# Batch 0's convolution moved right behind its own top-k tiles, with its feed-forward beside the last four top-k tiles of batch 1

## The chip, the cores and the metric

One Trainium2 chip, one of its cores. The time is the device time of one execution in microseconds (us); lower is better.

## The reference

The model is two attention blocks and two expert blocks on a text of two batches of 1024 rows by 256 channels and a context of two batches of 77 rows by 192. Cut to what matters here (the first attention and the first expert block, called A and B below, are not touched except for B's last step):

```python
x = x + xattn0(x, ctx)                       # A: 16 heads
x = x + experts0(x)                          # B: top 2 of 8, gated, projected by Wo
# C: 4 heads over 77 keys, the 32 largest scores of each row kept
scores = einsum(Q, K) / sqrt(32)
topv, topi = top_k(scores, 32); probs = softmax(topv)
c_t = attn.mean(heads) @ V                   # FiLM: scale and shift in and out
u = layernorm(x);  x_in = u * (1 + scale_in) + shift_in
# D: long convolution over the 1024 rows, by Fourier transform
y = irfft(rfft(x_in) * rfft(K)) + x_in * D_skip
# FiLM out, layernorm, then E: gelu(h @ W1 + b1) @ W2 + b2, layernorm, residual
# F: y = x @ w_expert + b ; gate by the largest of 8 logits, at most 100 rows per expert
```

(The names are shortened; the layer norms and residual sums around each block are as in the reference.)

## The kernel before

The kernel is written engine by engine: one list of instructions for each of PE (tensor), DVE (vector), ACT (scalar), POOL (gpsimd) and SP (DMA issue). Each list runs strictly in its written order, and waits on semaphores where it needs another engine's result. So the order of the calls in a list is the schedule, and an instruction whose wait has not come holds up all that stands behind it.

The 2048 rows are 16 tiles of 128 rows, 8 for each batch (`TB = 8`), and four blocks of 512 rows. All matrix products are in f32. The steps that the change and the prediction speak of, with their lines:

- End of B: for each tile, ACT takes half of a sum of two gathered expert rows (`half_sum`, L1229), DVE the other half (`sum_gated`, L1679), PE turns it (`turn_sum`, L778) and multiplies by `wof` (`out_B`), ACT copies the turned tile in between (`put_sumT`), and DVE adds it to X (`add_B`, L2083). These run `LEAD = 6` tiles ahead of the top-k loop.
- Preparation of C: PE makes four small products for the FiLM rows, then four for the keys (`wqk`); ACT copies the keys and DVE scales the FiLM rows (`film_rows`).
- C for tile n: PE `turn_u`, `scores`; DVE `top_k` as four rounds of `top_eight`, each of four MAX8 (L2137) and four MATCH_REPLACE8 (L2141), the end of the first round being a small L2148; ACT `exp_all` (L1272) and `exp_top_and_rest` (L1279, L1284); POOL `weights` (L1591 to L1604), which begins by inverting the sums of exponentials; PE `turn_attn` (L814) and `film_in`; ACT `put_attn` and `put_film`; POOL `x_in` (L1610, L1612).
- The spectrum of the convolution's kernel: 8 steps of PE `kernel_spectrum`, ACT `put_kernel`, DVE `kernel_pair` (L2154), through one PSUM bank, one step in each of the iterations 1 to 8.
- D for batch b: DVE `fold` (L2172); PE `spectra(b, pair)`, 8 products of 128x512; ACT `put_spectra`; DVE four `product` calls; PE `inverse(b, pair)`; DVE `unfold` (L2225); then PE `film_pair` and DVE `film_add` for each pair of tiles, which alternate; DVE `stats_E`, POOL `rstd_E`, ACT `norm_E`, PE `turn_E`.
- E for block i: PE `hidden(i, f)`, f = 0 to 7, ACT `gelu` (L1355), PE `out_E` for four tiles, DVE `add_E` and `norm_E`. Before E, PE makes `b1_folded` (16 products of one column) for the bias, once.
- F for block i: DVE `stats_F`, `norm_F`; PE `expert_F` (`turn_F`, `out_F`); ACT `put_zTF`; DVE `back_F`. Then the gate and the stores.

In the kernel before, batch 0's convolution is spread over the iterations 9 to 15 of the top-k loop. Block 0 of E follows the loop, then batch 1's convolution between the blocks 0 and 1, then the blocks 2 and 3 with the experts F of the blocks 0 and 1 beside them. In `weights(n)` POOL inverts four sums of exponentials as a power of -1:

```python
own.done(p.tensor_tensor(q_[:, 1, :], q_[:, 0, :], negone[:], ALU.pow))
```

## Time and profile before

| what | value |
|---|---|
| median of 3 runs | 857.21 us (855.03 to 858.87) |
| the profiled execution's own time | 865.67 us |
| span of the profiled execution | 863.6 us |
| mean granted TensorE clock | 0.886 of full speed |
| busy: PE, DVE, ACT, POOL | 690.4, 539.8, 343.3, 390.9 us |

The span is what the engines' instructions cover; the profiled execution took 2.1 us more than its span. A stretch of the profile gives for each engine its busy time and count, then the granted clock of TensorE as a share of full speed. PE's busy time is the time in which a product was under way, so a slower clock makes it larger. In the timeline each row has a start, a duration, the engine, the line, and in brackets how long the engine had stood idle before and whose result it had waited for. f32 products stand as two or more records each.

### The profile page before, as it was taken

Reading aid. Unit: us, or ns where it says so; the run is one execution under the profiler, and the core shown is the slowest. Engines: PE = TensorE matmul, PEld = TensorE weight load, DVE = VectorE, ACT = ScalarE, POOL = GpSimd, SP = SyncE. Lnnn points to the kernel's source line nnn. Section 1 sums busy time; section 2 is a strip of 40 time slices with the busy share of each in tenths; the row PEclk is TensorE's granted clock in tenths of the full one; section 3 lists DMA queues with packets and bytes.
Section 4 is the critical chain, followed back from the end, with each engine's and each line's share of the span. In section 5 each row is a group of like instructions: output and inputs, shape, how many; then the busy total and the mean of one; then the engine's idle time right before and its main releaser. Section 6 shows DMA issues by size and latency. Waiting matters only on the chain.

```text
span 863.6 us, 10795 instructions
## 1 busy us (share of the span) xinstructions
PE 690.4 (80%) x3380; PEld 387.4 (45%) x3380; DVE 539.8 (63%) x1641; ACT 343.3 (40%) x776; POOL 390.9 (45%) x448
## 2 busy tenths in 40 slices
PE   4798888369998989895688997827858997999972
PEld 2344455334454544442454544313513742657661
DVE  4889884749948393601568878598263476654165
ACT  2565553216373828210356765433334121042210
POOL 4666341238887877610126667655332410123020
PEclk9989998569999999986789999877757998999987
DMA  8920010211222222205930004000000000000002
GB/s 217 392 59 2 0 65 25 73 43 62 86 80 73 89 67 86 86 26 167 362 129 1 1 1 147 1 0 1 0 1 0 1 0 0 2 0 1 1 0 97
DMA packets 33215, 52.78 MB, mean 61 GB/s; under 512 B 8846, under 2 KB 21710, under 8 KB 32904
## 3 DMA queue, kind: packets, MB, share of 16 engines
q1 hardware_dynamic: 28168, 36.76, 12.9%
q0 software_dynamic: 4992, 15.34, 5.3%
q8 instruction: 28, 0.46, 0.2%
q14 instruction: 27, 0.22, 0.1%
HBM read 36.62 MB, written 15.47 MB: 60 GB/s over the span
## 4 chain that ended last, share of the span: by engine, by line
PE 47%; DVE 31%; ACT 10%; issue 6%; POOL 2%; DMA 1%; POOLq 1%; SPq 0%; DVEq 0%; ACTq 0%
PE ps L479 44%; DVE arena L1673 6%; DVE kp L1673 4%; DVE arena L1790 3%; DVE arena L1786 3%; DVE arena L1776 2%; ACT arena L1037 2%; ACT arena L1121 2%; DVE arena L2141 2%; ACT L1194 1%; DVE arena L2137 1%; DVE arena L2025 1%; DVE arena L340 1%; ACT L1208 1%; DVE arena L1676 1%
## 5 line engine op out<-in xcount | busy, mean ns | idle before, releaser
L479 PE MATMUL ps<-arena 64*32 64x32 f32 (+6 forms) x2280 | 480.9, 400 | 42.6 <-ACT arena L1037 11.7
L479 PEld LDWEIGHTS ps<-arena 128*128 128x128 f32 (+4 forms) x2280 | 221.9, 153 | 235.0 <-issue 172.9
L1037 ACT ACTIVATE arena<-ps 128x512 f32<-128x512 f32 (+4 forms) x228 | 108.1, 496 | 199.1 <-PE ps L479 114.3
L2025 DVE TENSOR_TENSOR arena<-ps,arena 128x512 f32<-128x512 f32 x39 | 26.9, 689 | 85.6 <-ACT arena L1194 77.4
L335 POOL TENSOR_SCALAR rstd<-mv 128x1 f32<-128x1 f32 (+1 forms) x24 | 10.8, 450 | 132.5 <-DVE mv L329 104.7
L1535 POOL DMA_INDIRECT scr_g<-arena,destU x39 | 48.8, 1252 | 44.1 <-DVE arena L2025 35.0
L1493 POOL TENSOR_TENSOR arena<-arena 128x616 f32<-128x616 f32 x32 | 39.0, 1217 | 50.5 <-DVE arena L1778 50.4
L1526 POOL DMA_INDIRECT arena<-scr_z,idsU x39 | 49.5, 1270 | 22.9 <-PE ps L708 11.6
L1673 DVE TENSOR_TENSOR arena<-arena 128x1024 f32<-128x1024 f32 (+10 forms) x47 | 40.3, 858 | 29.8 <-issue 18.5
L1194 ACT ACTIVATE arena<-ps 128x512 f32<-128x512 f32 x39 | 23.3, 598 | 83.7 <-PE ps L479 83.6
L2141 DVE MATCH_REPLACE8 arena<-arena 128x77 f32<-128x77 f32 x256 | 54.1, 222 | 0.0
L2137 DVE MAX8 arena<-arena 128x8 f32<-128x77 f32 x256 | 41.7, 224 | 16.7 <-POOL arena L1604 12.3
L1355 ACT ACTIVATE arena<-ps,b1p 128x512 f32<-128x512 f32 x32 | 22.0, 688 | 60.5 <-PE ps L479 60.5
L1591 POOL TENSOR_TENSOR arena<-arena,negone 128x4 f32<-128x4 f32 x16 | 21.7, 1354 | 53.9 <-ACT arena L1279 53.9
L479 PE MATMUL ps<-arena,wq 128*128 128x308 f32 (+1 forms) x104 | 40.0, 510 | 4.7 <-ACT arena L1037 4.1
L1121 ACT ACTIVATE arena<-arena 128x616 f32<-128x616 f32 x32 | 22.9, 717 | 45.5 <-DVE arena L1790 45.4
L479 PE MATMUL ps<-b1r,picked 72*128 72x512 bf16 x78 | 30.6, 393 | 8.7 <-DVE arena L2025 4.6
L479 PE MATMUL ps<-wof,arena 128*128 128x256 f32 x128 | 35.3, 425 | 0.6 <-DVE X L2083 0.5
L1673 DVE TENSOR_TENSOR arena<-arena,kp 128x1024 f32<-128x1024 f32 (+1 forms) x32 | 34.6, 1102 | 0.3
L1610 POOL TENSOR_TENSOR arena<-arena 128x256 f32<-128x256 f32 x16 | 12.8, 800 | 47.3 <-ACT arena L1037 47.3
L1776 DVE TENSOR_REDUCE arena<-arena 128x8 f32<-128x616 f32 x32 | 25.3, 791 | 13.4 <-ACT arena L1121 12.5
L814 PE MATMUL ps<-ident,arena 128*77 128x128 f32 x16 | 5.4, 335 | 33.7 <-POOL arena L1604 33.6
(215 smaller groups left out, 1096.8 us busy)
## 6 DMA issues: line engine op xcount, KB each, us to landing
arena<-in_w1t SPq DMA_DIRECT2D x8, 1024.0 KB, 14.7
arena<-scr_g SPq DMA_DIRECT2D x14, 512.0 KB, 5.9
X<-in_x SPq DMA_DIRECT2D x2, 1024.0 KB, 6.2
scr_z<-arena SPq DMA_DIRECT2D x4, 512.0 KB, 2.8
arena<-in_c_dftf SPq DMA_DIRECT2D x1, 2048.0 KB, 14.1
arena<-in_L_xattn_W SPq DMA_DIRECT2D x2, 1024.0 KB, 6.3
out<-X SPq DMA_DIRECT2D x16, 128.0 KB, 1.8
scr_k<-arena SPq DMA_DIRECT2D x4, 256.0 KB, 5.8
```

What stands on the lines that cost most here:

```text
L479: return pe.matmul(o, l, r, start=first, stop=final)
L1037: return a.activation(o, i, ACT.Copy)
L1121: a.activation(Pb[:, S % PBUF, :], Pb[:, S % PBUF, :], ACT.Exp, scale=1.0 / math.sqrt(DH0))\
L1194: a.activation(sig[:, u % 2, :], bank(2 * (u % 2) + 1), ACT.Sigmoid).then_inc(s["sig_ready"], 1)
L1493: p.tensor_tensor(pv, pv, smA[:, u % PBUF, :].unsqueeze(2).broadcast_to([P, HG, S2]), ALU.mult)\
L1526: p.indirect_dma_start(xg[:, st % 2, :], None, scr_z, bass.IndirectOffsetOnAxis(ap=idsU[:, st:st + 1], axis=0))\
L1535: p.indirect_dma_start(scr_g, bass.IndirectOffsetOnAxis(ap=destU[:, u:u + 1], axis=0), gt[:, u % 2, :], None).then_inc(s[f"gs{u % 2}"], 16)
L1673: own.done(v.tensor_tensor(o, x, y, op))
L1776: own.done(v.tensor_reduce(smA[:, u % PBUF, :], Pb[:, u % PBUF, :].rearrange("p (h k) -> p h k", h=HG), AX, ALU.add))
L2025: v.tensor_tensor(gt[:, u % 2, :], bank(2 * (u % 2)), sig[:, u % 2, :], ALU.mult).then_inc(s["g_ready"], 1)
L2137: own.done(v.max(top[:, par, h, 8 * r:8 * r + 8], hv(cur)[:, h, :]))
L2141: ins = v.match_replace(hv(Rr)[:, h, :], top[:, par, h, 8 * r:8 * r + 8], hv(cur)[:, h, :], TAKEN)
```

## The change

It changes the order of the calls on PE, ACT, POOL and DVE from the end of B on, and moves buffers and PSUM banks so that the new order has no clash:

- PE's loop goes over the tiles 0 to 9 and the rest is written out. `kernel_spectrum(n)` stands in iteration n (0 to 7), behind `turn_attn(n-1)`. Tiles 12 to 15 of B's end (`EARLY = 12`) come after tile 8's top-k.
- After tile 10's top-k come all four products of batch 0 in a row, then tile 11, unfold and FiLM of batch 0; block 0 of E runs beside the top-k of the tiles 12 to 14, block 1 beside tile 15 and ahead of batch 1's convolution.
- F of the blocks 0 and 1 stands between batch 1's spectra. ACT, not DVE, takes F's results from PSUM (`put_yF`), and POOL adds the bias (`bias_F`).
- The inverse of the sums of exponentials moves from POOL (`negone`, pow) to DVE (`invert`, a reciprocal of 128x4), which signals `ex_inv`.
- On ACT the first two `half_sum` stand ahead of the copies of `wqk`.
- `hidden` goes round three PSUM banks instead of two, and `xT` has two buffers.

```diff
@@ tensor @@
                 for n in range(NT):
                     if n + 1 < NT:
                         scores(n + 1)
-                    if n + LEAD + 1 < NT:
+                    if n + LEAD < EARLY:
                         turn_sum(n + LEAD + 1)
-                    if n + LEAD < NT:
                         out_B(n + LEAD)
-                    if 1 <= n <= 8:
-                        kernel_spectrum(n - 1)
                     if n:
                         turn_attn(n - 1)
+                    if n < 8:
+                        kernel_spectrum(n)
...
+                    if n == 8:
+                        out_B(EARLY)
+                        turn_sum(EARLY + 1)
+                        out_B(EARLY + 1)
                     if n == 9:
                         spectra(0, 0)
...
+                        break
+                turn_sum(EARLY + 2)
+                out_B(EARLY + 2)
+                turn_attn(9)
+                scores(11)
+                film_in(9)
+                turn_sum(EARLY + 3)
+                out_B(EARLY + 3)
+                spectra(0, 1)
+                turn_attn(10)
+                film_in(10)
+                inverse(0, 0)
+                turn_u(12)
+                scores(12)
+                b1_folded()
+                inverse(0, 1)
...
@@ scalar @@
+                half_sum(0)
+                half_sum(1)
                 for b in range(NB):
                     for g in range(2):
                         a.wait_ge(s["prepC_ps"], 8 + 2 * b + g)
                         copy(wqk[:, g, b, :], bank((4, 5, 1, 7)[2 * b + g], SW)).then_inc(s["prepC_sb"], 1)
-                half_sum(0)
-                half_sum(1)
...
+                for n in range(8):
                     exp_all(n)
+                    put_scores(n + 1)
+                    if n + LEAD < EARLY:
                         put_sumT(n + LEAD + 1)
                         half_sum(n + LEAD + 3)
                     if n:
                         put_attn(n - 1)
+                    if n in (2, 6):
+                        norm_u(n // 4 + 1)
+                    exp_top_and_rest(n)
+                    put_kernel(n)
                     if n:
                         put_film(n - 1)
+                    put_uT(n + 2)
...
+                exp_all(12)
+                gelu(0, 0)
+                gelu(0, 1)
+                put_scores(13)
+                put_uT(14)
+                gelu(0, 2)
+                gelu(0, 3)
+                exp_top_and_rest(12)
+                exp_all(13)
+                gelu(0, 4)
...
@@ gpsimd @@
                 def weights(n):
 
                     q_, E = smC[:, n % 2], Ex[:, n % 2, :]
-                    p.wait_ge(s["ex_sum"], n + 1)
-                    own.done(p.tensor_tensor(q_[:, 1, :], q_[:, 0, :], negone[:], ALU.pow))
-                    own.settle()
+                    p.wait_ge(s["ex_inv"], n + 1)
...
@@ vector @@
+                def invert(n):
+
+                    v.wait_ge(s["ex_sum"], n + 1)
+                    v.reciprocal(smC[:, n % 2, 1, :], smC[:, n % 2, 0, :]).then_inc(s["ex_inv"], 1)
+
+                for n in range(8):
+                    top_k(n, (0, 1))
+                    if n + LEAD + 2 < EARLY + 2:
                         sum_gated(n + LEAD + 2)
+                    if n:
+                        invert(n - 1)
+                    top_k(n, (2, 3))
+                    if n + LEAD < EARLY:
                         add_B(n + LEAD)
+                    kernel_pair(n)
+                top_k(8, (0, 1))
+                sum_gated(14)
+                invert(7)
+                add_B(12)
+                top_k(8, (2, 3))
+                sum_gated(15)
+                add_B(13)
+                kernel_ends()
+                invert(8)
+                top_k(9, (0, 1))
+                fold(0)
+                top_k(9, (2, 3))
+                top_k(10, (0, 1))
+                invert(9)
+                top_k(10, (2, 3))
+                add_B(14)
+                invert(10)
+                product(0, 0, 0)
+                add_B(15)
+                product(0, 0, 1)
+                product(0, 1, 0)
+                product(0, 1, 1)
...
```

How the instructions stand. First PE in one iteration of the loop (`L778` or `L780` is turn_sum, `wof` out_B, the row of 128x512 x4 is kernel_spectrum, `L814` or `L816` turn_attn, `L796` or `L798` turn_u, `L479` arena 128x512 alone film_in, `onerow` and `wq` scores). Before:

```order
L479 MATMUL ps<-arena,onerow 128x308
L479 MATMUL ps<-arena,wq 128x308 x2
L778 MATMUL ps<-ident,arena 128x128 x4
L479 MATMUL ps<-wof,arena 128x256 x4
L479 MATMUL ps<-arena 128x512 x4
L814 MATMUL ps<-ident,arena 77x128
L796 MATMUL ps<-ident,arena 128x128 x2
L479 MATMUL ps<-arena 128x512
```

and of the change:

```order
L479 MATMUL ps<-arena,onerow 128x308
L479 MATMUL ps<-arena,wq 128x308 x2
L780 MATMUL ps<-ident,arena 128x128 x4
L479 MATMUL ps<-wof,arena 128x256 x4
L816 MATMUL ps<-ident,arena 77x128
L479 MATMUL ps<-arena 128x512 x5
L798 MATMUL ps<-ident,arena 128x128 x2
```

The four products of the kernel's spectrum now stand behind turn_attn, and film_in follows them directly (five products of 128x512 in a row).

Second, DVE in one tile of the loop in the change (`L2291` and `L2295` are the top-k rounds, `L1833` sum_gated, `L2407` invert, `L2237` and `L2239` add_B, `L2308` kernel_pair):

```order
L2302 TENSOR_SCALAR arena<-arena 128x4
L2291 MAX arena<-arena 128x8 x4
L2295 MATCH_REPLACE arena<-arena 128x77 x4
L1833 SCALAR_TENSOR_TENSOR arena<-arena,cw 128x512
L2407 RECIPROCAL arena<-arena 128x4
L2291 MAX arena<-arena 128x8 x4
L2295 MATCH_REPLACE arena<-arena 128x77 x4
L2291 MAX arena<-arena 128x8 x4
L2295 MATCH_REPLACE arena<-arena 128x77 x4
L2237 TENSOR_TENSOR X<-X,ps 128x256
```

The inverse for tile n-1 stands behind two rounds of tile n, and kernel_pair, which stood between the rounds 3 and 4, is now the last of the tile.

Third, ACT beside block 0 of E in the change (`L1407` is gelu, `L1333` and `L1338` exp_top_and_rest, `L1326` exp_all):

```order
L1326 ACTIVATE arena<-arena 128x77 x4
L1407 ACT_TABLE_LOAD
L1407 ACTIVATE arena<-ps,b1p 128x512 x2
L1317 ACTIVATE arena<-ps 128x308
L1091 ACTIVATE wq<-ps 128x256
L1407 ACTIVATE arena<-ps,b1p 128x512 x2
L1333 ACT_TABLE_LOAD
L1333 ACTIVATE arena<-arena 128x32 x4
L1338 ACTIVATE arena<-arena 128x77 x4
L1326 ACTIVATE arena<-arena 128x77 x4
L1407 ACT_TABLE_LOAD
```

Gelu and exponentials now alternate. From tile 12 on seven loads of a table stand between them, where before there was one.

## Rows read from the trace of the kernel before

**Rows 1.** Page: busy time of each engine; the chain that ended last; gathers to landing
```profile
PE 690.4 (80%) x3380; PEld 387.4 (45%) x3380; DVE 539.8 (63%) x1641; ACT 343.3 (40%) x776; POOL 390.9 (45%) x448
...
PE 47%; DVE 31%; ACT 10%; issue 6%; POOL 2%; DMA 1%; POOLq 1%; SPq 0%; DVEq 0%; ACTq 0%
...
arena<-scr_g SPq DMA_DIRECT2D x14, 512.0 KB, 5.9
```

**Rows 2.** Windows: PE, PEld, DVE, ACT, POOL busy (count), PE clock, DMA share, GB/s
```profile
480.00:500.00 20.00, 19.08 (x67) 10.39 (x65) 17.12 (x126) 13.16 (x51) 12.43 (x22) 1.00 0.00 1
560.00:580.00 20.00, 7.22 (x22) 3.17 (x20) 19.90 (x67) 6.99 (x25) 10.07 (x10) 0.78 0.00 0
...
620.00:640.00 20.00, 12.72 (x32) 7.21 (x32) 10.94 (x56) 4.96 (x16) 5.42 (x9) 0.50 0.01 1
```

**Rows 3.** Timeline of ACT before the loop: copies of wqk, then the first half sums
```profile
412.38 1.98 ACT L1037 ACTIVATE arena<-ps 128x308 f32<-128x308 f32 x4 [10.11 <-PE ps L479]
414.26 1.32 ACT L1229 ACTIVATE arena<-arena,cw 128x512 f32<-128x512 f32 x2
```

**Rows 4.** Timeline of DVE before the loop: sums 0 and 1, sum 2, first round of top-k
```profile
415.00 1.41 DVE L1679 SCALAR_TENSOR_TENSOR arena<-arena,cw 128x512 f32<-128x512 f32 x2 [13.07 <-ACT arena L1229]
...
424.66 0.75 DVE L1679 SCALAR_TENSOR_TENSOR arena<-arena,cw 128x512 f32<-128x512 f32 x1 [0.22 <-DVE arena L1676]
...
445.76 0.66 DVE L2137 MAX8 arena<-arena 128x8 f32<-128x77 f32 x4 [4.31 <-ACT arena L1263]
```

**Rows 5.** Timeline of PE before the loop: the products for the FiLM rows
```profile
402.32 9.50 PE L479 MATMUL ps<-arena 128*77 128x512 f32 x16 [0.39 <-ACT arena L1037]
```

**Rows 6.** Timeline of DVE in the loop: tile 2's rounds, ends of round 1, tile 7's kernel_pair
```profile
460.93 0.63 DVE L2137 MAX8 arena<-arena 128x8 f32<-128x77 f32 x4
...
463.76 0.74 DVE L1679 SCALAR_TENSOR_TENSOR arena<-arena,cw 128x512 f32<-128x512 f32 x1
...
472.32 0.16 DVE L2148 TENSOR_SCALAR arena<-arena 128x4 f32<-128x4 f32 x1
...
481.54 0.16 DVE L2148 TENSOR_SCALAR arena<-arena 128x4 f32<-128x4 f32 x1
...
534.76 0.41 DVE L2154 TENSOR_TENSOR arena<-ps,arena 128x256 f32<-128x256 f32 x1
```

**Rows 7.** Timeline of POOL in the loop: first and last step of weights behind the inverse
```profile
477.21 0.30 POOL L1593 TENSOR_SCALAR arena<-arena 128x4 f32<-128x4 f32 x1
...
479.71 0.32 POOL L1604 TENSOR_TENSOR arena<-arena 128x77 f32<-128x77 f32 x1
```

**Rows 8.** Timeline of PE: kernel_spectrum, turn_attn, b1_folded, a film_pair at low clock
```profile
477.17 3.60 PE L479 MATMUL ps<-arena 128*128 128x512 f32 x8
480.61 0.27 PE L814 MATMUL ps<-ident,arena 128*77 128x128 f32 x1
...
618.00 6.83 PE L479 MATMUL ps<-gb_ffn,arena 128*128 128x1 f32 x32
...
629.95 3.78 PE L479 MATMUL ps<-arena 97*128 97x512 f32 x4 [1.50 <-DVE kp L2235]
```

**Rows 9.** Groups of ACT behind 445 us, forms apart: copies of 128x256, mean ns
```profile
L1037 ACT ACTIVATE arena<-ps 128x256 f32<-128x256 f32 x40 | 15.2, 379 | 44.0 <-PE ps L928 27.1 <-PE ps L479 16.9
```

**Rows 10.** Timeline of DVE: fold(0), first and last step of two products of batch 1
```profile
531.09 2.36 DVE L2172 TENSOR_TENSOR arena<-arena 128x1024 f32<-128x1024 f32 x2 [1.88 <-POOL arena L1612]
...
717.97 1.23 DVE L1673 TENSOR_TENSOR arena<-arena 128x1024 f32<-128x1024 f32 x1 [6.71 <-issue]
...
729.64 0.69 DVE L2215 TENSOR_TENSOR arena<-arena,kp 128x512 f32<-128x512 f32 x1
```

**Rows 11.** Timeline of ACT in block B: a table load between two functions
```profile
250.85 0.38 ACT L1037 ACTIVATE arena<-ps 128x256 f32<-128x256 f32 x1
251.25 1.28 ACT L1208 ACT_TABLE_LOAD   x1
252.54 1.06 ACT L1208 ACTIVATE arena<-arena 128x1024 f32<-128x1024 f32 x1
```

602 lines of the change are left out of this document (343 added, 259 removed).

## The prediction

> **What bounds the kernel now.** I read the page first: PE is busy for 80% of the span but holds only 47% of the chain that ended last, DVE 31% [rows 1]. So there are stretches of two kinds, and the windows tell them apart [rows 2]. In the top-k loop (480 to 500 us) PE is busy 19.1 of 20 us at full clock: PE is the bound. From about 550 to 655 us it is not. At 560 DVE is busy 19.9 of 20 us with batch 0's products while PE has 7.2, and at 620 PE's granted clock is 0.50 (its 1.2 GHz level). The change aims at this second stretch. Whether it pays depends on what the new order does to the first. So I took the timelines and followed, in each engine's new list, which wait ends last, with durations from the rows.
>
> **The change, part by part.** Times are in the profiled execution, whose span is 863.6 us (its own time is 865.67, 1% above the median of 857.21; I carry the difference in us over to the median).
>
> *Ahead of the loop: a gain of 8 us.* ACT copies the keys at 412.4, when PE has made the last of its eight products, and only then takes the first half sums at 414.3 [rows 3]. DVE therefore starts its sums 0 and 1 at 415.0, and its FiLM rows stand behind them: sum 2 comes at 424.7 [rows 4]. With the half sums first, they need only the first gathers, which land 5.9 us after their issue [rows 1], at about 405. DVE then does the FiLM rows while PE still makes them (402.3 to 411.8 [rows 5]), and should be through at 416.3. The first round of top-k moves from 445.8 [rows 4] to about 437.5.
>
> *The loop: a new ring of waits, 11.3 us a tile in place of 9.2.* Before, a tile takes 481.54 - 472.32 = 9.2 us [rows 6], about PE's work. In the change this ring closes:
> - DVE ends kernel_pair(n-1), the last of its tile, and does two rounds of tile n: 463.76 - 460.93 = 2.83; sum_gated 0.7 [rows 6]; then invert(n-1), which I take at 0.25 (no such row; the small L2148 takes 0.16 [rows 6], and twice my value is the upper end).
> - POOL's weights(n-1) without the power: 477.21 to 480.03, 2.82 [rows 7].
> - PE's turn_attn(n-1), 0.2 until the next can start, and behind it kernel_spectrum(n), 3.60 [rows 8].
> - ACT's copy 0.38 [rows 9], DVE's kernel_pair(n) 0.41 [rows 6], and some 0.2 for the handoffs.
>
> The sum is 11.35 us. Before, kernel_spectrum stood ahead of turn_attn and waited for no weights. Seven turns of the ring give 79.4. The first tile has about 10.5 us (two exponential groups stand ahead of its copy), norm_u in two of the tiles adds 1.9, and the tiles 6 and 7, which have no gated sum, give back 1.4. Tile 7's kernel_pair then ends 90.2 us after the first round, at 527.7. Before it ended at 535.2 [rows 6], but with tile 8's top-k and half of tile 9's behind it, and with four steps of B that now still stand ahead. The power that POOL no longer takes is no gain here: its place in the ring is taken by two rounds of top-k.
>
> *From there to block 0 of E: 107 us.* I count from tile 7's kernel_pair.
> - Tile 8: DVE's add_B(12) waits for out_B(12), which stands behind turn_attn(7) and film_in(7): 11.2. Its other two rounds end at 14.9. ACT's put_sumT(13) is behind tile 8's exponentials, so out_B(13) ends at 21. kernel_ends and two rounds of tile 9 take it to 26.7, fold 2.36 [rows 10] to 29.3.
> - PE's spectra(0,0), 6.9 at full clock, come after a nearly idle stretch: 9.5, to 38.8. Then put_sumT(14), out_B(14), turn_attn(9), scores, film_in(9), put_film and tile 10's sum stand in one line over ACT and PE: invert(10) at 48.6.
> - Four products. Two with one op of 0.4 between them span 717.97 to 730.33, so 6.0 each [rows 10]. With add_B(15) and a wait of 0.4 they end at 74.2.
> - PE: inverse(0,0) to 71, scores, b1_folded 6.8 [rows 8] to 79, inverse(0,1) 6.9 to 86, unfold to 89.3. Tile 11's top-k is hidden in it.
> - film_pair and film_add alternate four times. A pair takes 1.8 at full and 3.78 at the 1.2 GHz level [rows 8], an add three ops of 0.69 like the last of a product [rows 10]. With stats_E, norm_E and turn_E ahead of the last pair that is 17.7 at a mean between the levels. `hidden(0)` starts at 107, at 634.7 us.
>
> *The blocks 0 and 1 of E: 66.4 us to out_E(4), then 52.2 us to the last product of batch 1.* PE has 18.2 us of work in block 0's hidden part, but ACT's list has norm_E(1), the exponentials of tiles 12 and 13 and three table loads in it: 26.4. Block 1 stands twice behind put_attn, which is behind a gelu. The six added loads cost 1.28 each, at once behind the op before and with the next at once behind them [rows 11], so 7.7 in all, nearly all of it in ACT's full stretches. The Trainium skill, "ScalarE: Activation LUTs", section "Table sets: the hidden batching unit", gives the rule to batch calls by table set, which speaks against this interleaving. Its section on the cost states 2.66 us for a switch with its drain, by which six would be 16 us; here a load with both neighbours spans 1.31, so the sum goes by 1.28.
> Then out_E(4 to 7) 15, spectra(1,0) 7, and the products, which wait for put_spectra(1,1) behind the third yf_ready: the last ends 225.6 after tile 7's pair, at 753.3. Before it ended at 730.3 [rows 10], but with out_E(4 to 7) and the experts F of the blocks 0 and 1 still to do.
>
> *The end: 121.2 us in place of 133.3.* inverse(1,0) stands behind expert_F(1), so 9.8 to its end, unfold, four film pairs with PE nearly idle: hidden(2) 28 after the last product. Blocks 2 and 3 with expert_F(2) take 62.3. The tail from the last out_E I put at 31, some 5 shorter than before, since F's last block no longer queues behind DVE's back_F of the block before.
>
> *Sum:* 437.5 + 90.2 + 107 + 66.4 + 52.2 + 121.2 = 874.5, or 10.9 over 863.6. On the median: **868 us**.
>
> **Costs at nothing.** POOL's added bias_F, a sum of 128x256 each, runs while ACT and PE do the next tile; only if rstd_E(2) queued behind the first eight would it cost, up to 3 us. Waiting for the table of the Fourier transform with the kernel's (`k_in`) is hidden: it was issued at 412 and POOL asks for it behind 434.
>
> **The rivals.**
> - *The order holds PE busy (faster).* If PE's clock stays at 2.4 GHz from 550 on and the table loads fall into ACT's waits, the sum loses 15 (low clock: spectra 2.6, out_B 2, inverses and b1 3, film pairs 4 + 3) and 8: 851.5, on the median 845. For it: PE has some 59 us of work in the 107 and 91 in the 118 after. Against: in the like stretch before the clock was 0.78 and 0.50 [rows 2], and the film pairs leave PE half idle. The break-even with before is at 11 of these 23 us.
> - *Half of that (no change):* only the clock or only the loads: 853 to 861, hardly any of it above.
> - *The loop throttles as well (slower still).* In the ring PE works 8.8 (19.1 / 20 of 9.2 [rows 2, 6]) of 11.3 us. If the clock fell there, kernel_spectrum at 1.2 GHz would add up to 3.4 to a turn; over half the tiles that is 12: 880. Against: the gaps are short.
> - *The ring doesn't bind,* because weights(n-1) is ready sooner than I read. Then the loop keeps 9.2 a tile, 15 us less: 853. The written order leaves no way for it that I see.
>
> **How the numbers follow.** The sum as it stands, with its walk uncertain by some 9 us: 0.50. PE held busy: 0.18. Half of it: 0.15. The loop throttled too: 0.11. Ring not binding: 0.06. The range reaches from 845, the first rival, to 882, which takes in the third rival and invert at twice its cost; about 2 in 10 lie outside. A measurement of this kernel tells 0.5% (4.3 us) from no change, so slower means over 861.5, faster under 852.9. The sum's case puts 0.40 above, 0.07 between and 0.03 below; with the rivals: slower 0.53, same 0.20, faster 0.27.
>
> **What would show it.** Right: kernel_pair rows 11.3 us apart, each waiting for ACT's copy; the first MAX8 of the loop at about 437; seven table loads between gelu and exponentials; hidden(0) at about 635; the last product of batch 1 at about 753; a clock well under 1.00 between 535 and 640. Wrong: kernel_pair rows 9 us apart, or a clock of 0.95 and more from 550 to 640, or a last product before 740.

## The result, and the profile after

The change takes **898.52 us** (median of 4 runs, 897.92 to 902.57; a fifth execution on record took 907.14) beside 856.12 us for the kernel before: ratio 1.052, 95% interval 1.046 to 1.058. The prediction said 868 us with a range to 882. The direction was right and the size was not: 42 us were lost, not 11.

The profiled execution, page: busy times, granted clock in 40 slices, the chain that ended last.

```profile
PE 699.5 (78%) x3380; PEld 389.0 (43%) x3380; DVE 534.4 (59%) x1625; ACT 360.4 (40%) x814; POOL 383.9 (43%) x448
...
PEclk9999996589999999969899877976789897889986
...
PE 45%; DVE 30%; ACT 14%; issue 5%; POOL 4%; DMA 1%; POOLq 1%; SPq 0%; DVEq 0%; ACTq 0%
```

Against [rows 1] nearly no work was added (PE 9 us, ACT 17), the span grew by 37, and what gained in the chain is ACT, from 10% to 14%. So time was lost in waits, and ACT is in them.

First a correction of the scale. The last step ahead of stage C is a drain of POOL's DMA queue. The chain of waits before, then after:

```profile
390.79 7.66 POOLq L320
```

```profile
381.24 7.65 POOLq L320
```

Stage C began at 398.5 before and at 388.9 in the change, though nothing ahead of it is altered. In 14 of the 19 profiles of this study it begins between 388.6 and 391.9, in the other five (before, ring_open2, warm_all, no_tables, before_warm) between 398.5 and 409.3. In these five the granted clock from 360 to 380 was 0.74 to 0.92, in the others 1.00. The last four ran on one chip, on which the kernel before took 867.43 us and not 856 to 857, so a late stage C isn't the kernel's doing. The profile before was a late one, which is why its own time stood 1% above its median. I therefore count **from the start of stage C** (the end of that drain). From there the span is 465.1 us before and 511.8 in the change: 46.7 more. A second profile of the change (run `again`) gave 512.0, every landmark of it within 2.2 us. How far a single profile can be trusted stands under `again`.

Ahead of the loop, timelines of ACT (half sums, then the copies of wqk) and DVE (sums 0 and 1, first round of top-k), against [rows 3, 4]:

```profile
394.40 1.34 ACT L1283 ACTIVATE arena<-arena,cw 128x512 f32<-128x512 f32 x2 [1.68 <-DMA arena<-scr_g]
402.24 1.98 ACT L1091 ACTIVATE arena<-ps 128x308 f32<-128x308 f32 x4 [6.51 <-PE ps L479]
```

```profile
395.15 1.42 DVE L1833 SCALAR_TENSOR_TENSOR arena<-arena,cw 128x512 f32<-128x512 f32 x2 [2.78 <-ACT arena L1283]
...
426.60 0.66 DVE L2291 MAX8 arena<-arena 128x8 f32<-128x77 f32 x4 [5.21 <-ACT arena L1317]
```

The first round comes 37.7 us behind the start of C (426.6 - 388.9), before 47.3: a gain of 9.6.

In the loop, DVE's kernel_pair of the tiles 4 to 7:

```profile
485.63 0.42 DVE L2308 TENSOR_TENSOR arena<-ps,arena 128x256 f32<-128x256 f32 x1 [3.63 <-ACT arena L1091]
496.96 0.43 DVE L2308 TENSOR_TENSOR arena<-ps,arena 128x256 f32<-128x256 f32 x1 [3.21 <-ACT arena L1091]
510.45 0.42 DVE L2308 TENSOR_TENSOR arena<-ps,arena 128x256 f32<-128x256 f32 x1 [7.24 <-ACT arena L1091]
524.02 0.42 DVE L2308 TENSOR_TENSOR arena<-ps,arena 128x256 f32<-128x256 f32 x1 [7.32 <-ACT arena L1091]
```

They wait for ACT's copy, as forecast, and two of the turns are 11.33 us to the hundredth. But the last two are 13.5, the first three 12.9, 12.3 and 13.0, and the mean over all seven is (524.02 - 436.15) / 7 = 12.55. PE's rows tell why: turn_attn with its wait, and behind it kernel_spectrum and film_in, in a fast turn and in a slow one.

```profile
492.74 0.34 PE L816 MATMUL ps<-ident,arena 128*77 128x128 f32 x1 [1.89 <-POOL arena L1727]
492.91 4.46 PE L479 MATMUL ps<-arena 128*128 128x512 f32 x10
...
503.43 0.49 PE L816 MATMUL ps<-ident,arena 128*77 128x128 f32 x1 [3.41 <-POOL arena L1727]
503.72 7.15 PE L479 MATMUL ps<-arena 128*128 128x512 f32 x10
```

The same ten records take 4.46 or 7.15 us. Windows of the change, against [rows 2]:

```profile
480.00:500.00 20.00, 14.92 (x48) 7.76 (x48) 13.05 (x95) 11.43 (x45) 11.37 (x22) 1.00 0.00 0
500.00:520.00 20.00, 12.29 (x24) 5.62 (x24) 9.46 (x79) 10.29 (x41) 7.97 (x14) 0.73 0.01 1
560.00:580.00 20.00, 15.20 (x47) 8.92 (x47) 13.03 (x48) 9.49 (x37) 11.25 (x13) 0.91 0.09 31
620.00:640.00 20.00, 14.82 (x25) 5.59 (x25) 7.87 (x17) 4.17 (x9) 6.32 (x12) 0.59 0.00 0
```

From 480 to 500 PE is busy 14.9 us, where it had been 19.1. In the next window the granted clock is 0.73: the order that was to take PE's waits out of the second half put waits into the loop too, and the clock fell there. It fell in four of the seven turns, those in which PE had stood 2.7 to 3.4 us ahead of turn_attn, and not in the three with 1.9 us. But 1.9 us is not safe either. In the second profile, `again`, the same ten records, in turn 4, stand behind a wait of 1.90 and take 6.16:

```profile
484.40 0.33 PE L816 MATMUL ps<-ident,arena 128*77 128x128 f32 x1 [1.90 <-POOL arena L1727]
484.57 6.16 PE L479 MATMUL ps<-arena 128*128 128x512 f32 x10
```

Beside block 0 of E, ACT's and PE's timelines (L1407 is gelu, L1333 to L1326 exponentials, L1294 norm_E, L905 turn_E):

```profile
657.08 1.09 ACT L1326 ACTIVATE arena<-arena 128x77 f32<-128x77 f32 x4
658.18 1.28 ACT L1407 ACT_TABLE_LOAD   x1
659.47 0.69 ACT L1407 ACTIVATE arena<-ps,b1p 128x512 f32<-128x512 f32 x1
...
660.63 2.08 ACT L1294 ACTIVATE arena<-arena,rstd 128x256 f32<-128x256 f32 x4
...
666.32 0.69 ACT L1407 ACTIVATE arena<-ps,b1p 128x512 f32<-128x512 f32 x1 [2.79 <-PE ps L479]
```

```profile
661.78 1.11 PE L905 MATMUL ps<-ident,arena 128*128 128x128 f32 x4 [5.56 <-ACT arena L1294]
662.69 5.31 PE L479 MATMUL ps<-arena 128*128 128x512 f32 x8
```

PE stands 5.56 us behind ACT's exponentials, load and norm_E, begins at the low clock (5.31 for eight records that take 3.71 elsewhere), and now ACT waits 2.79 for it. Each engine's queue makes the other late.

### The profile page after: what moved, and what is told of

Its sections match the earlier page's. It is cut to its first block, busy times and chain, and to the rows that moved or that the text cites. A ratio compares the mean times of both kernels' runs of the same rounds, so it can differ in the third digit from the quotient of the medians.

```text
span 900.7 us, 10807 instructions
## 1 busy us (share of the span) xinstructions
PE 699.5 (78%) x3380; PEld 389.0 (43%) x3380; DVE 534.4 (59%) x1625; ACT 360.4 (40%) x814; POOL 383.9 (43%) x448
## 3 DMA queue, kind: packets, MB, share of 16 engines
q1 hardware_dynamic: 28168, 36.76, 12.3%
## 4 chain that ended last, share of the span: by engine, by line
PE 45%; DVE 30%; ACT 14%; issue 5%; POOL 4%; DMA 1%; POOLq 1%; SPq 0%; DVEq 0%; ACTq 0%
PE ps L479 42%; DVE arena L1827 5%; DVE kp L1827 3%; DVE arena L1944 3%; ACT arena L1091 2%; DVE arena L1940 2%; DVE arena L1930 2%; DVE arena L2295 2%; ACT arena L1175 2%; DVE arena L2291 1%; ACT L1248 1%; DVE arena L2179 1%; DVE X L1833 1%; ACT L1262 1%; POOLq L320 1%
## 5 line engine op out<-in xcount | busy, mean ns | idle before, releaser
L479 PE MATMUL ps<-arena 64*32 64x32 f32 (+6 forms) x2280 | 485.7, 403 | 43.4 <-ACT arena L1091 14.9
L479 PEld LDWEIGHTS ps<-arena 128*128 128x128 f32 (+4 forms) x2280 | 224.1, 154 | 241.1 <-issue 168.2
L1091 ACT ACTIVATE arena<-ps 128x512 f32<-128x512 f32 (+5 forms) x260 | 115.9, 469 | 213.6 <-PE ps L479 98.2
L1651 POOL DMA_INDIRECT arena<-scr_z,idsU x39 | 49.5, 1268 | 23.0 <-PE ps L708 11.6
L2295 DVE MATCH_REPLACE8 arena<-arena 128x77 f32<-128x77 f32 x256 | 54.0, 221 | 0.0
L1716 POOL TENSOR_SCALAR arena<-arena 128x4 f32<-128x4 f32 x16 | 7.0, 435 | 98.4 <-DVE arena L2407 98.4
L2291 DVE MAX8 arena<-arena 128x8 f32<-128x77 f32 x256 | 41.3, 221 | 6.6 <-ACT arena L1317 6.6
L479 PE MATMUL ps<-arena,wq 128*128 128x308 f32 (+1 forms) x104 | 40.9, 520 | 4.7 <-ACT arena L1091 4.1
L479 PE MATMUL ps<-wof,arena 128*128 128x256 f32 x128 | 35.1, 423 | 12.0 <-ACT arena L1091 11.2
L2465 DVE TENSOR_TENSOR arena<-arena,ps 128x256 f32<-128x256 f32 x16 | 6.7, 420 | 61.9 <-PE ps L479 61.7
L1407 ACT ACTIVATE arena<-ps,b1p 128x512 f32<-128x512 f32 x32 | 21.9, 687 | 47.7 <-PE ps L479 47.7
L479 PE MATMUL ps<-b1r,picked 72*128 72x512 bf16 x78 | 30.1, 386 | 8.8 <-DVE arena L2179 4.8
L479 PEld LDWEIGHTS ps<-wof,arena 128*128 128x128 f32 x128 | 25.9, 213 | 17.6 <-ACT arena L1091 12.1
## 6 DMA issues: line engine op xcount, KB each, us to landing
arena<-scr_g SPq DMA_DIRECT2D x14, 512.0 KB, 6.6
scr_z<-arena SPq DMA_DIRECT2D x4, 512.0 KB, 2.8
```

What stands on the lines that cost most here:

```text
L479: return pe.matmul(o, l, r, start=first, stop=final)
L1091: return a.activation(o, i, ACT.Copy)
L1651: p.indirect_dma_start(xg[:, st % 2, :], None, scr_z, bass.IndirectOffsetOnAxis(ap=idsU[:, st:st + 1], axis=0))\
L2291: own.done(v.max(top[:, par, h, 8 * r:8 * r + 8], hv(cur)[:, h, :]))
L2295: ins = v.match_replace(hv(Rr)[:, h, :], top[:, par, h, 8 * r:8 * r + 8], hv(cur)[:, h, :], TAKEN)
```

## The experiments

All counts are from the start of stage C in each run's profile; the ratio is to runs of the kernel before on the same chip, with its 95% interval. The columns after it are the starts of the first round of top-k's rows, tile 7's kernel_pair, the second step of film_add(3), add_E(4), and the end.

| run | ratio | first round | pair 7 | film_add(3) | add_E(4) | end |
|---|---|---|---|---|---|---|
| before | 1 | 47.3 | 136.3 | 253.4 | 344.3 | 465.1 |
| half_first | 0.991 (0.987 to 0.994) | 37.7 | 126.1 | 242.2 | 333.0 | 453.9 |
| the change | 1.052 (1.046 to 1.058) | 37.7 | 135.1 | 254.0 | 331.1 | 511.8 |
| again | 1.052 (1.047 to 1.056) | 37.7 | 135.6 | 254.1 | 331.3 | 512.0 |
| ring_open | 1.048 (1.046 to 1.050) | 37.7 | 130.4 | 251.7 | 325.4 | 503.0 |
| ring_open2 | 1.022 (1.019 to 1.024) | 37.7 | 107.8 | 227.7 | 301.5 | 479.0 |
| warm_loop | 1.048 (1.045 to 1.051) | 37.7 | 131.2 | 251.7 | 325.5 | 503.1 |
| warm_all | 1.042 (1.039 to 1.044) | 37.7 | 131.8 | 246.9 | 322.3 | 501.6 |
| warm_loop2 | 1.041 (1.040 to 1.043) | 37.7 | 127.5 | 248.2 | 322.0 | 499.6 |
| warm_all2 | 1.019 (1.017 to 1.020) | 37.7 | 127.6 | 231.6 | 302.0 | 479.4 |
| gelu_first | 1.044 (1.042 to 1.046) | 37.7 | 135.5 | 255.0 | 327.5 | 503.9 |
| no_tables | 1.034 (1.031 to 1.036) | 37.7 | 133.1 | 252.5 | 314.7 | 491.1 |
| fill | 1.050 (1.048 to 1.053) | 37.7 | 135.3 | 254.2 | 328.1 | 507.5 |
| ring2_no_tables | 1.002 (1.001 to 1.004) | 37.7 | 107.7 | 227.7 | 289.9 | 466.4 |
| combo | 1.015 (1.013 to 1.018) | 37.7 | 107.7 | 227.6 | 300.2 | 476.7 |
| best_a | 0.994 (0.992 to 0.995) | 37.7 | 107.7 | 213.8 | 283.5 | 458.8 |
| before_warm | 0.995 (0.992 to 0.998) | 37.7 | 126.5 | 247.2 | 337.6 | 458.3 |
| before_warm2 | 0.984 (0.981 to 0.988) | 37.7 | 131.1 | 241.3 | 330.0 | 450.6 |
| best_b | 0.976 (0.974 to 0.979) | 37.7 | 126.1 | 233.1 | 322.8 | 443.6 |

(add_E(4) stands behind batch 1's products in the order of before, ahead of them in the change's.)

### How well a profile repeats: again

> The change as it is, once more. In the profiles so far stage C begins at 389 to 409 us, though nothing ahead of it is altered, so spans are compared from its first product on: 511.8 us in the change. This run tells how well that repeats: 508 to 514 from there if it is a steady measure, more apart if not.

512.0 against 511.8. But two profiles don't tell how far executions spread. Up to tile 7's kernel_pair the change, `again`, gelu_first, no_tables and fill have the same code, and it stands at 133.1 to 135.6. The orders of before have the same code there in half_first, before_warm, before_warm2 and best_b, and it stands at 126.1 to 131.1. And executions of the change that took 897.3 to 897.9 us can't have spent 511.8 behind a start of stage C at 388.6, the earliest seen; 507.5 is the most. So I take a difference in the table as real when it is over 5 us, or when the ratios bear it out.

### The prologue alone: half_first

The kernel before with one edit:

```diff
+                half_sum(0)
+                half_sum(1)
                 for b in range(NB):
                     for g in range(2):
...
-                half_sum(0)
-                half_sum(1)
```

> The kernel before with one edit: the first two half_sum on ACT ahead of the copies of wqk, as in the change. If the prologue's gain is this alone and reaches the end: 8 to 9.7 us less than before, 847. Rival (the loop waits in its first tiles for something else, like the B steps that run ahead): less than 3 us, 854.

The median is 847.40 beside 855.96. The first round comes at 37.7 as in the change, and the whole gain reaches the end (the profile shows 11.2, the medians 8.6). This part of the change is good by itself.

### The ring of the loop: ring_open, ring_open2

```diff
+                    if n < 8:
+                        kernel_spectrum(n)
                     if n:
                         turn_attn(n - 1)
-                    if n < 8:
-                        kernel_spectrum(n)
...
+                    put_kernel(n)
                     exp_top_and_rest(n)
-                    put_kernel(n)
```

> The change with one edit: in the tiles 0 to 7 kernel_spectrum(n) stands ahead of turn_attn(n-1) on PE, and put_kernel(n) ahead of exp_top_and_rest(n) on ACT. Theory 1 (the ring over kernel_pair, weights, turn_attn and kernel_spectrum sets the loop's pace): without it PE's own work of about 9.2 us is the bound, so kernel_pair rows come 9.2 to 9.6 apart in place of 12.55 on average, tile 7's kernel_pair ends some 75 us after the first round in place of 98, and of these 23 us at least 18 reach the end: 875 to 882. Rival (the loop is slow because PE's clock falls, whatever the order): the rows stay over 11 apart and the time at 890 or more.

The theory as I had it fell: the median is 897.25, by the ratios 4 us under the change with intervals that overlap (its profile, 503.0, shows 9), and the turns are 11.9 on average, (522.30 - 439.18) / 7. The timelines of PE and ACT in a turn at full clock (L816 turn_attn; the ACT rows are put_attn, put_uT and the next put_attn) show what took over:

```profile
492.60 0.30 PE L479 MATMUL ps<-arena,onerow 1*128 1x308 bf16 x1 [2.03 <-ACT wq L1091]
...
496.14 3.60 PE L479 MATMUL ps<-arena 128*128 128x512 f32 x8
499.58 0.27 PE L816 MATMUL ps<-ident,arena 128*77 128x128 f32 x1
```

```profile
488.90 0.54 ACT L1091 ACTIVATE arena<-ps 77x128 f32<-77x128 f32 x2 [5.45 <-PE ps L816]
...
492.17 0.38 ACT L1091 ACTIVATE wq<-ps 128x256 f32<-128x256 f32 x1
...
499.88 0.54 ACT L1091 ACTIVATE arena<-ps 77x128 f32<-77x128 f32 x2 [4.07 <-PE ps L816]
```

There are **two rings of nearly one length**. ACT waits 5.45 us for PE's turn_attn, then does the exponentials and the film copies, and put_uT (492.17) last; PE's scores wait for put_uT. Scores, turn_sum, out_B, kernel_spectrum and turn_attn take PE to 499.8, and ACT starts again. That turn is 499.88 - 488.90 = 10.98 us, 0.35 under the one I had found, and since it holds all of PE's work it should grow more when the clock falls (the run has turns of 12.7 and 14.6 besides, and a clock of 0.91 in the windows from 440 to 500). ring_open2 opens this one too. PE gets the order that before had, and ACT takes the copies ahead of the exponentials (against the change; norm_u, which moves with them, is left out here):

```diff
+                    if n < 8:
+                        kernel_spectrum(n)
                     if n:
                         turn_attn(n - 1)
-                    if n < 8:
-                        kernel_spectrum(n)
+                    if n + 2 < EARLY:
+                        turn_u(n + 2)
                     if n:
                         film_in(n - 1)
-                    if n + 2 < EARLY:
-                        turn_u(n + 2)
...
+                    put_kernel(n)
...
                         put_attn(n - 1)
...
-                    exp_top_and_rest(n)
-                    put_kernel(n)
+                    put_uT(n + 2)
                     if n:
                         put_film(n - 1)
-                    put_uT(n + 2)
+                    exp_top_and_rest(n)
```

> The run ring_open left a second ring: ACT's put_attn(n-1) stood ahead of the exponentials and put_uT(n+2) of tile n, and PE's scores(n+2) waits for that copy, so PE and ACT took turns (10.98 us a tile at full clock). This kernel opens both rings: PE makes kernel_spectrum(n), turn_attn(n-1), turn_u(n+2), film_in(n-1) in this order, and ACT put_kernel(n), put_attn(n-1), put_uT(n+2), put_film(n-1) and only then exp_top_and_rest(n). Theory 1b (two rings of nearly one length): kernel_pair rows 9.2 to 9.8 apart, tile 7's kernel_pair some 20 us sooner than in the change; with most of it at the end 880 to 885. Rival (B's steps 12 to 15 and the walk behind tile 7 are bound by something else): the pairs come sooner, and the end by less than 8 us.

```profile
479.40 0.42 DVE L2308 TENSOR_TENSOR arena<-ps,arena 128x256 f32<-128x256 f32 x1 [1.77 <-ACT arena L1091]
488.22 0.42 DVE L2308 TENSOR_TENSOR arena<-ps,arena 128x256 f32<-128x256 f32 x1 [0.93 <-ACT arena L1091]
497.05 0.42 DVE L2308 TENSOR_TENSOR arena<-ps,arena 128x256 f32<-128x256 f32 x1 [0.51 <-ACT arena L1091]
```

DVE's kernel_pair rows now stand 8.8 us apart (8.6 on average), with hardly a wait, and the clock is 1.00 in the windows from 460 to 500. Tile 7's kernel_pair comes 27.3 us sooner (107.8 against 135.1), and all of it is kept: 32.8 less at the end, or 0.030 of before by the ratios, 26 us. The turns are shorter than the 9.2 to 9.8 that I had expected. This is one of the two largest gains of a single cause (the other is the clock, next), and the two overlap: in ring_open2 the loop also ran at full clock.

### PE's clock: warm_loop, warm_all, before_warm and their second forms

PE gets products that nobody reads, in the time in which it waits:

```diff
+                def warm(k):
+                    for _ in range(k):
+                        mm(ps[:, 3, P:P + D], ident[:], wof[:, 0, :], True, True)
...
+                    if n and n < 8:
+                        warm(6 if n < 6 else 12)
                     if n:
                         turn_attn(n - 1)
```

> The change with products added that nobody reads: in tile n of the loop, ahead of turn_attn(n-1), PE makes 6 of 128x256 (tiles 1 to 5) or 12 (tiles 6 and 7), some 1.5 and 3 us, in time in which it waited. They lengthen nothing in the ring. Theory 2 (PE's clock falls to its lower level behind its idle stretches, and that alone makes the turns 13 us in place of 11.33): the granted clock is 1.00 from 440 to 525, all turns are about 11.3, tile 7's kernel_pair ends 8 us sooner: 890. Rival (the clock doesn't follow PE's idle time, or it falls from work): clock and turns as in the change or worse, 898 or more.

> warm_loop's products and more of the same kind behind the loop: 14 ahead of turn_attn(7) and (8), 22, 5 and 10 ahead of out_B(13) to (15), 18 ahead of film_in(10), 12, 5 and 5 ahead of the film pairs 0 to 2, 6 and 20 ahead of turn_E(0, 0) and (1, 0), 10 ahead of film_in(13) and (14). Theory 2 (the low clock behind idle stretches costs what the prediction's first rival counted, 15 us behind the loop): the granted clock is 0.95 and more from 440 to 700, film pairs take 1.8 to 2.0 us in place of 3.78, and the time is 13 to 19 us under the change's: 880 to 885. Rival (these stretches are bound by chains over ACT and DVE, which hide PE's slowness, and added products come late for some): 4 us less or fewer, 894 or more.

> half_first (the kernel before with the first half sums ahead of the copies of wqk) and products that nobody reads where PE waits in the iterations 12 to 15: 56, 10, 8 and 26 of 128x256 ahead of turn_attn(11) to (14), 5 each between film_pair(0) and (1), and (2) and (3), 12 ahead of hidden(0, 0). Theory 2: the clock stays near 1.00 from 545 to 640, the film pairs and b1_folded take half their time, and the time is 8 to 12 us under half_first's 847.4: 836 to 840. Rival (DVE's products and adds bound this stretch): within 3 us of 847.

These three gave little. warm_loop had the clock at 1.00 from 440 to 520 as forecast, and yet turns of 12.0; warm_all's clock from 440 to 700 was 0.98 and its gain 9 us by the ratios, not 13 to 19; before_warm's profile was 4.4 us longer than half_first's (the intervals of their ratios overlap). The timeline of PE in before_warm shows the error, which was mine:

```profile
562.43 24.34 PE L479 MATMUL ps<-wof,ident 128*128 128x256 f32 x112
```

The 56 products took 24.3 us, 0.43 each, where I had assumed 0.24 (each stands as two records, and I had taken a record for a product); they were to fill a wait of 15.5. The fill held the work up. With counts by the measured 0.43 the same places give another answer:

> warm_loop with fewer products, sized by their measured 0.43 us each: 4 (1.7 us) in the tiles 1 to 5 and 8 (3.5 us) in 6 and 7, within PE's waits. Theory 2: clock 1.00 in the loop and turns of 11.33 except the two with norm_u, so tile 7's kernel_pair stands 128 to 130 us behind the start of stage C (135.1 in the change, 131.2 in warm_loop) and the time is 5 to 8 us under the change's, ratio to before 1.043 to 1.047. Rival (warm_loop's gain was all that the clock has to give): 131 or more.

> warm_all with the counts halved (8, 8; 13, 3, 6 ahead of out_B(13) to (15); 10 ahead of film_in(10); 7, 3, 3 ahead of the film pairs 0 to 2; 4 and 11 ahead of turn_E(0, 0) and (1, 0); 6 and 6 ahead of film_in(13) and (14)), each within the wait of the change. Theory 2: beyond warm_loop2's gain another 10 to 15 us, so 487 to 495 from stage C's start against 511.8. Rival (chains over ACT and DVE hide PE's slowness behind the loop): 500 or more, as warm_all.

> before_warm with counts within the waits: 33, 6, 5 and 15 ahead of turn_attn(11) to (14), 3 between the film pairs, 7 ahead of hidden(0, 0), on half_first (453.9 from stage C's start). Theory 2: film pairs at 2 us in place of 3.8 and b1_folded at 3.5 in place of 6.8: 443 to 447. Rival: DVE's and ACT's chains bound it, within 3 us of 453.9.

In warm_loop2 the clock is 1.00 in every window from 440 to 520, and tile 7's kernel_pair stands at 127.5, 7.6 us sooner; the ratios give 0.011, 9 us. warm_all2 gained more than I had expected, 479.4 for 487 to 495. Its windows, beside those of the change above:

```profile
500.00:520.00 20.00, 17.62 (x61) 10.40 (x59) 10.22 (x82) 10.51 (x42) 7.98 (x14) 1.00 0.04 3
...
620.00:640.00 20.00, 18.19 (x61) 10.11 (x61) 15.25 (x110) 12.75 (x32) 4.50 (x10) 1.00 0.00 1
```

And PE's timeline at the film pairs of batch 0, first the change, then warm_all2:

```profile
619.61 3.78 PE L479 MATMUL ps<-arena 97*128 97x512 f32 x4 [3.55 <-DVE kp L2379]
```

```profile
606.07 1.98 PE L479 MATMUL ps<-arena 97*128 97x512 f32 x4 [0.53 <-DVE kp L2405]
607.89 1.46 PE L479 MATMUL ps<-wof,ident 128*128 128x256 f32 x6
609.55 1.98 PE L479 MATMUL ps<-arena 97*128 97x512 f32 x4 [0.20 <-DVE kp L2415]
```

A pair takes 1.98 us in place of 3.78. In all, work without a use makes the change 32.4 us faster (511.8 to 479.4; by the ratios 0.033 of before, 28 us): its median is 872.66. The two differ in nothing else, so this is the price of the low clock as far as the added products removed it (in batch 1's part, where none stand, it still falls at times in both). It is about twice the 15 that I had in the sum.

The kernel before has the same loss in smaller measure. before_warm2's median is 843.57. Its profile, 450.6, missed the 443 to 447 expected: tile 7's kernel_pair stands 5 us later than in half_first, in a stretch where the two kernels are the same. The clock fell there, to 0.85 from 480 to 500 where half_first had 1.00; why in the one execution and not in the other isn't shown. So the stretch with the fill gained more than the end shows.

### The gelus and the table loads: gelu_first, no_tables, fill

```diff
-                exp_all(12)
                 gelu(0, 0)
...
+                exp_all(12)
                 exp_top_and_rest(12)
...
-                exp_all(15)
                 gelu(1, 0)
...
+                exp_all(15)
                 exp_top_and_rest(15)
```

> The change with exp_all(12) and exp_all(15) on ACT moved from ahead of gelu(0, 0) and gelu(1, 0) to ahead of the exponentials of the same tile that follow four gelus later. The number of table loads stays. Theory 3 (the gelus of block 0 and 1 wait for DVE's round of a top-k that they don't need): gelu(0, 0) starts 5 to 8 us sooner, the exponentials of tile 12 then wait for its fourth round and give most of it back, and block 1 keeps 3 to 5 us: 892 to 894. Rival (what sets these blocks is PE's work at a low clock): within 2 us of the change.

894.44, just above the range: 4 us by the medians, 7 by the ratios. The load ahead of gelu(0, 0) starts 7.6 us sooner (252.3 against 259.9), but in block 0 nothing comes of it (add_E(0) at 287.5, as in the change); the 3.6 us at add_E(4) are block 1's.

```diff
-                    a.activation(hT[:, f, :], bank(H_BANK[f % 3]), ACT.Gelu, bias=b1p[:, f:f + 1])
+                    a.activation(hT[:, f, :], bank(H_BANK[f % 3]), ACT.Gelu if i > 1 else ACT.Identity, bias=b1p[:, f:f + 1])
```

> The change with the gelu of the blocks 0 and 1 replaced by Identity with the same bias (hidden values without gelu in these blocks), so that six of the seven table loads go. Theory 4 (each load costs its 1.28 us in ACT's full stretches, as the prediction's sum has it): 6 to 8 us less, 891 to 893. Rival a (ACT waits for PE's slow products there): less than 2 us, 897. Rival b (a switch costs 2.66 us with its drain): 14 to 16 us, 884.

> no_tables (Identity in place of gelu in the blocks 0 and 1, so no loads there; 491.1 from stage C's start) with four copies of 128x256 on ACT, some 1.3 us in all, at each of the seven places where a load stood. Theory 4b (a load costs the 1.28 us that its row shows, and the rest of no_tables' 20 us comes from what that delay starts: PE waits, and its clock falls): from stage C's start as in the change, 506 to 513. Rival (a load holds ACT longer than its row shows): well below, 492 to 500.

Without the loads it is 491.1, 20.7 less (0.018 of before by the ratios, 16 us): more than six rows of 1.28, which are 7.7 (seven go, and one comes back ahead of gelu(2, 0)). 1.5 of the 20.7 stand there already at film_add(3), ahead of the edit. fill tells whether a load holds ACT longer than its row. Four copies stand in the place of a load:

```profile
655.43 1.46 ACT L1091 ACTIVATE kp<-arena 128x256 f32<-128x256 f32 x4
656.80 0.30 ACT L1333 ACTIVATE arena<-arena 128x32 f32<-128x32 f32 x1
```

They take 1.37 to the next row, and with them the time is back at 507.5 (899.33 as median): 16.4 of the 20.7 return with plain copies of a load's length. The last 4.3 us between fill and the change are within what two profiles differ by, and the ratios (1.050 and 1.052) don't tell the two apart. So as far as this tells, a load holds ACT no longer than its row, and the rest is what that delay sets off.

What it sets off shows between film_add(3) and add_E(4), where all seven loads lie. The windows of the change, fill and no_tables there:

```profile
643.00:720.00 77.00, 61.18 (x181) 34.10 (x180) 35.67 (x238) 40.29 (x107) 28.29 (x45) 0.89 0.00 1
```

```profile
645.00:719.00 74.00, 58.56 (x181) 33.31 (x180) 35.88 (x239) 39.89 (x128) 28.30 (x45) 0.93 0.00 1
```

```profile
662.00:724.00 62.00, 55.70 (x180) 32.08 (x179) 36.02 (x239) 30.41 (x100) 28.21 (x45) 0.97 0.00 1
```

The change takes 77.1 us at a clock of 0.89, fill 73.9 at 0.93, no_tables 62.2 at 0.97, for the same products. warm_all2, which has the seven loads and a clock of 1.00 there, takes 70.4. So of the 14.9 us that the loads cost there, 8.2 remain when the clock is held, about the 9.0 of their rows, and 6.7 are the clock that falls behind the waits they make.

### Do the causes add up: ring2_no_tables, combo, best_a, best_b

> ring_open2 (479.0 from stage C's start) and no_tables (491.1) together; no gelu in the blocks 0 and 1. If the rings and the loads are two causes that add up: 458 to 463 from there, against 465.1 of before and 453.9 of half_first, so the new placement of batch 0's stages itself costs only some 7 against half_first. If they overlap: 470 or more.

466.4, between the two: 12.6 below ring_open2 where the loads alone had been worth 20.7. By medians it is 857.90 beside 856.57, so without both, the new order is the old one's equal, though without gelu in two blocks. Against half_first, which has the same gain ahead of the loop, it is still 12.5 us longer (10 by the ratios), not some 7: the new placement itself costs that much.

combo kept the gelu and regrouped ACT's list instead:

```diff
-                exp_all(12)
                 gelu(0, 0)
...
                 gelu(0, 3)
-                exp_top_and_rest(12)
-                exp_all(13)
+                norm_E(1)
                 gelu(0, 4)
...
                 gelu(0, 7)
+                put_xT(1, 1)
+                exp_all(12)
+                exp_top_and_rest(12)
+                exp_all(13)
```

> A version meant to be faster: ring_open2, with ACT's list beside block 0 regrouped (all eight gelus and norm_E(1) first, then the exponentials of tile 12 and exp_all(13)), turn_E(1, 0) and (1, 1) on PE behind hidden(0, 5) and hidden(0, 7), scores(14) behind out_E(1), and in block 1 exp_all(15) behind the fourth gelu: two loads fewer, and no product of block 0 behind an exponential. Theory: 8 to 12 us less than ring_open2's 479.0 from stage C's start, 467 to 471. Rival (DVE's top-k of the tiles 12 to 14, ahead of add_E(0), then bounds the block, and the later exponentials make it later): 476 or more.

476.7, only 2.3 under ring_open2 (5 by the ratios): the rival. Two loads fewer and gelus in one row, but the first of the tile-12 exponentials is later, and DVE's and PE's timelines show where the time stays:

```profile
641.86 0.66 DVE L2291 MAX8 arena<-arena 128x8 f32<-128x77 f32 x4 [2.69 <-ACT arena L1316]
```

```profile
648.12 10.02 PE L479 MATMUL ps<-arena 128*128 128x256 f32 x34 [6.48 <-DVE arena L2465]
```

DVE's top-k of tile 14 stands ahead of add_E(0), waits for ACT, and PE's out_E waits 6.48 us for add_E.

best_a joins ring_open2's loop, gelu_first's order and warm_all2's products behind the loop, with 18 more in batch 1's part. best_b is before_warm2 with nearer counts:

```diff
-                    if n >= 12:
-                        warm((33, 6, 5, 15)[n - 12])
+                    if n == 9:
+                        warm(8)
+                    elif n >= 12:
+                        warm((37, 9, 5, 15)[n - 12])
...
-                warm(7)
+                warm(10)
```

> The change with ring_open2's order in the loop, warm_all2's products behind it (8 ahead of turn_attn(7) and (8) and the rest as there, none in the loop), gelu_first's order of exponentials, and products also in batch 1's part: 8 ahead of expert_F(1), 3, 3 and 4 behind film_pair(4), (5) and (6). If the causes are separate: 479.4 of warm_all2 less 19.8 (tile 7's kernel_pair at 107.8 in place of 127.6), less 3 to 4 for gelu_first and 2 to 4 for batch 1's film pairs, so 452 to 455 from stage C's start and 0.983 to 0.99 of before. If they overlap: 462 or more.

> before_warm2 with counts nearer to the waits that it left: 8 ahead of turn_attn(8), 37, 9, 5 and 15 ahead of turn_attn(11) to (14), 10 ahead of hidden(0, 0). 446 to 449 from stage C's start (450.6 in before_warm2), 0.978 to 0.983 of before. Rival (what is left of the waits costs no clock, or the longer fill comes late): 450 or more.

best_a: 851.48 us, 458.8 from stage C, 4 to 7 more than if all had added up, so the causes overlap only a little here. The new order, cured, is a shade faster than before (0.994), but not than half_first (0.991). **best_b beats both kernels: 836.97 us, 0.976 of before** (0.974 to 0.979), with two edits: the half sums first and 90 products that nobody reads. Its windows beside half_first's own, from the same places of the program:

```profile
560.00:580.00 20.00, 18.65 (x67) 11.67 (x65) 19.90 (x99) 6.40 (x26) 12.74 (x14) 1.00 0.01 1
...
600.00:620.00 20.00, 19.41 (x61) 12.88 (x61) 12.50 (x65) 8.04 (x25) 8.52 (x14) 0.81 0.01 1
```

```profile
560.00:580.00 20.00, 12.89 (x26) 5.54 (x26) 19.90 (x93) 6.45 (x26) 13.38 (x14) 0.71 0.00 0
...
600.00:620.00 20.00, 11.15 (x35) 7.21 (x35) 10.62 (x55) 4.90 (x16) 5.34 (x9) 0.59 0.00 0
```

The clock is 1.00 and 0.81 where it was 0.71 and 0.59.

## Why the prediction was wrong in size

The sum had five stretches, from the first round on. Measured in the change and, for the clock's part, in warm_all2:

| stretch | predicted | the change | warm_all2 |
|---|---|---|---|
| first round to tile 7's kernel_pair | 90.2 | 97.8 | 90.3 |
| to hidden(0) | 107 | 117.5 | 102.7 |
| to out_E(4) | 66.4 | 74.3 | 67.6 |
| to batch 1's last product | 52.2 | 56.5 | 56.8 |
| to the end | 121.2 | 127.9 | 124.4 |
| sum | 437.0 | 474.1 | 441.7 |

(hidden(0) starts behind film_pair(3), at 641.96 and 622.02; out_E(4) at 716.29 and 689.61; the last product ends at 772.82 and 746.37. The prediction's terms for the loop add up to 11.39 a turn and 90.4 in all where it has 11.35 and 90.2, which changes nothing below.)

The sum was 37 us short. **The term that failed most is the low clock**: the sum had 15 us for it (2.6, 2, 3, 4 and 3), nothing of it in the loop or in the blocks 0 and 1, and holding the clock gave 32.4. Without the clock's 15 the sum is 422.4, and warm_all2 took 441.7; so the other 19 us are terms that were too small even with the clock held.

- **Ahead of the loop: right.** Predicted 8, measured 9.6, and alone it is worth 8.6 at the end. The first round also came 9.5 us sooner than the profile before let expect, since that profile's stage C was itself late; it hid part of the loss in the change's span.
- **The loop: mechanism right, size off by 7.6, and that is the clock.** The ring is there, 11.33 us where the sum had 11.35, and with a steady clock the seven turns and the first tile give 90.3 for the 90.2. What failed is the step by which I gave the rival "the loop throttles as well" 0.11, "the gaps are short". PE's waits before turn_attn, 2.7 to 3.4 us and in `again` once 1.9, were enough: the clock was 0.91 from 440 to 480 and 0.73 from 500 to 520. The rival's price for the loop, 12, was more than the 7.5 measured; its 880 fell short because the terms behind the loop were too small. That a second ring lay 0.35 us under the first I had not seen; it cost the change nothing, but whoever opens one ring alone gets hardly anything for it.
- **The walk to hidden(0): 117.5 for 107, in three terms.** The clock took 14.8 where the sum had 11.6. The four products took 30.3 from invert(10) to their end, with the clock held too, where the sum had 25.6: I had priced each at 6.0 by a pair of batch 1 beside which POOL did nothing, and they took 7.6, 6.1, 7.1 and 6.0, with a wait of 2.2 for put_spectra in place of 0.4. And from the end of unfold the film pairs took 16.0 with the clock held, where the sum without its clock's 4 has 13.7.
- **The blocks 0 and 1: loads right by their rows, and the clock at nothing.** With the clock held the stretch took 67.6 for the 66.4, with 7.7 for the loads in it; in the change it took 74.3, because PE, which waits for ACT's loads and exponentials, comes back at the low level (the 5.31 of above). So taking the loads away gave 20.7 from stage C, 16 by the ratios. The Trainium skill, "ScalarE: Activation LUTs", section "What ACT_TABLE_LOAD costs", has the figure with a drain that I set aside; it would have made the sum 16. It is nearer to the effect, yet not by what it describes: fill shows that plain copies of a load's length bring most of it back, and every row of a load here is 1.28, with the next operation right behind it. The rule of its section "Table sets: the hidden batching unit", to batch by table set, holds here.
- **Batch 1's products: 4.5 too short, clock or no clock.** Here a cost that I put at nothing stands beside them: POOL's bias_F. DVE's steps of a product take 1.2 us where POOL is idle and up to 1.74 beside bias_F, whose four sums take 4.30, and the four products take 28.3 in place of 24:

```profile
752.96 1.74 DVE L1827 TENSOR_TENSOR arena<-arena,kp 128x1024 f32<-128x1024 f32 x1
```

```profile
750.98 4.30 POOL L1766 TENSOR_TENSOR arena<-arena,rows 128x256 f32<-128x256 f32 x4
```

Every slow step of a product in this profile ran beside POOL's work, but not every step beside it was slow, and no run takes bias_F away. So this is argued, not shown.
- **The end: 6.7 too long**, 3.2 with the clock held. The tail behind the last out_E took 33.4 and 34.0 for the 31; hidden(2) came 31.3 behind the last product for the 28, and 28.2 in warm_all2.
- **The rivals.** "The order holds PE busy" was the wrong way round: the order lets PE wait in more places than before. "The ring doesn't bind" is excluded by the 11.33.

The clock alone, at the 28 us of the ratios or the 32.4 of the profiles in place of 15, would have taken the 868 to some 882 or 886, the upper end of the range; the rest of the way to 898.5 is the other terms.

As for what the Trainium skill says of it: "TensorE: Matmul & The Clock Gate", in "HAM oscillation — how this bites in real kernels", tells of a kernel whose products stand between waits, so that each piece starts at the low clock, and advises to build the loop so that they don't. That is what the rows here show, with f32 products between waits for POOL and ACT in place of DMA. I had weighed only the page on tables against the trace, and this is the one that decided.

What stays open: why the clock was low from 360 to 380 in the five profiles with a late stage C (in two of them, ring_open2 and no_tables, it was 0.79 and 0.83 from 240 to 260 too, in the others of the five 1.00); whether bias_F slows the products; and what the other parts of the change are worth by themselves (the inverse on DVE, the copies of F on ACT, the third bank of hidden), which no run tests alone.
